# Another order of the projection units in a step of a graph attention kernel

## The reference

```python
h = relu(layernorm(x))
q, k, v = h @ Wq + bq, h @ Wk + bk, h @ Wv + bv          # 12 heads of 32
scores = q @ k^T / sqrt(32) + beta * adj                  # per graph and head, 128 x 128
scores = where(adj > 0, scores, -9e15)
out = x + softmax(scores) @ v
```

## Time and profile before

| | us |
|---|---|
| median of 3 runs | 1061.97 (1061.64 to 1063.23) |
| the profiled execution | 1062.6 |
| its span, first to last instruction | 1060.7 |
| TensorE busy | 1021.5 (96%) |
| TensorE weight loads busy | 710.6 (67%) |
| VectorE busy | 967.8 (91%) |
| ScalarE busy | 878.6 (83%) |
| GpSimd busy | 568.1 (54%) |
| mean granted TensorE clock | 0.987 of full |

### The profile page before, as it was taken

How to read it: one execution, slowest core, us unless ns; L and a number is a source line. 1 busy time by engine, 2 the same in 40 slices (tenths; PEclk the granted TensorE clock), 3 DMA queues, 4 the chain that set the end, 5 groups by cost and what they waited for, 6 DMA issues and landing times. The chain is left out here.

```text
span 1060.7 us, 33776 instructions
## 1 busy us (share of the span) xinstructions
PE 1021.5 (96%) x10959; PEld 710.6 (67%) x10959; DVE 967.8 (91%) x4343; ACT 878.6 (83%) x2343; POOL 568.1 (54%) x756
## 2 busy tenths in 40 slices
PE   3899999999999999999999999999999999999986
PEld 1466676776676776666777666677667677666664
DVE  6579999999999999999999999999999999999887
ACT  3378888888888888888888888888888888888887
POOL 3655655445656445565444565544565644566431
PEclk9899999999999999999999999999999999999997
DMA  4454445544455554445554444555444555445441
GB/s 158 102 132 115 131 131 146 160 131 130 106 138 139 160 138 133 111 131 139 153 144 132 109 139 131 149 149 139 132 111 131 142 160 138 131 105 138 110 121 39
DMA packets 91038, 138.79 MB, mean 131 GB/s; under 512 B 15600, under 2 KB 66288, under 8 KB 90864
## 3 DMA queue, kind: packets, MB, share of 16 engines
q1 hardware_dynamic: 90336, 135.85, 47.6%
q10 hardware_dynamic: 528, 0.79, 0.2%
HBM read 35.91 MB, written 25.17 MB: 58 GB/s over the span
## 5 line engine op out<-in xcount | busy, mean ns | idle before, releaser
L523 ACT ACTIVATE probs<-biased,neg_max 128x128 f32<-128x128 f32 x1536 | 490.3, 391 | 135.9 <-DVE neg_max L638 105.1
L437 PE MATMUL ps_p<-hT,w 128*128 128x512 f16 x1728 | 423.8, 382 | 6.4 <-DVE qT L619 4.2
L638 DVE CUSTOM_DVE_ANT_0 biased<-ps_s,mask 128x128 f32<-128x128 f32 x1536 | 353.4, 286 | 58.7 <-PE ps_s L458 57.0
L336 POOL TENSOR_TENSOR on<-on,xb 128x384 f32<-128x384 f32 x128 | 128.2, 1002 | 363.2 <-DVE on L659 362.4
L437 PEld LDWEIGHTS ps_p<-hT,w 128*128 128x128 f16 x1728 | 167.7, 98 | 158.1 <-DVE hT L609 8.2
L644 DVE TENSOR_TENSOR pT<-ps_t,pT 128x512 f16<-128x512 f32 x384 | 263.3, 686 | 0.9 <-ACT pT L548 0.9
L466 PE MATMUL ps_t<-ident,probs 128*128 128x128 f32 x1536 | 246.2, 283 | 0.1
L548 ACT ACTIVATE pT<-ps_t 128x512 f16<-128x512 f32 x384 | 220.8, 575 | 1.0 <-PE ps_t L466 1.0
L437 PE MATMUL ps_p<-w,hT 128*128 128x384 f16 x1152 | 207.6, 326 | 0.0
L458 PEld LDWEIGHTS ps_s<-k_st,q_st 96*128 96x128 f16 x1536 | 117.9, 97 | 81.4 <-DVE neg_max L638 6.7
L481 PE MATMUL ps_o<-v,pT 128*128 128x33 f16 x1536 | 157.3, 179 | 8.6 <-DVE pT L644 4.9
(11 more groups left out here) (62 smaller groups left out, 1016.9 us busy)
## 6 DMA issues: line engine op xcount, KB each, us to landing
q_st<-qT SPq DMA_DIRECT2D x384, 96.0 KB, 2.2
k_st<-kT SPq DMA_DIRECT2D x384, 96.0 KB, 2.2
out<-on SPq DMA_DIRECT2D x128, 192.0 KB, 2.1
xs<-in_x SPq DMA_DIRECT2D x31, 768.0 KB, 4.8
adjs<-in_adj SPq DMA_DIRECT2D x32, 256.0 KB, 5.1
xs<-in_x ACTq DMA_DIRECT2D x1, 768.0 KB, 7.2
k_st<-in_L_gnn_Wq SPq DMA_DIRECT2D x1, 576.0 KB, 5.4
k_st<-in_L_gnn_Wk SPq DMA_DIRECT2D x1, 576.0 KB, 9.4
```

The lines of the kernel that those rows point to most:

```text
L336: pool.tensor_tensor(on[:, j % 2, :], on[:, j % 2, :], xb[:, par, j, :], ALU.add).then_inc(added, 1)
L437: mm = pe.matmul(dst, stationary, moving, start=m == 0, stop=m == MMS - 1)
L523: act.activation(probs[:, odd, i, :], biased[:, odd, i, :], ACT.Exp, bias=neg_max[:, odd, i:i + 1], scale=-1.0).then_inc(exp_done, 1)
L638: dve.tensor_tensor_reduce(out=biased[:, odd, i, :], in0=ps_s[:, i * N:(i + 1) * N], in1=mask[:, gp, v // CH, :], scale=-1.0, scalar=3.0e3 ...
```

## The change

```diff
-    UNITS = ([("q", c) for c in range(CH)] + [(kind, c) for c in range(CH) for kind in ("k", "turn")]
-             + [("v", j) for j in range(G)])
+    UNITS = ([("q", c) for c in range(CH)] + [("k", 0), ("k", 1), ("turn", 0), ("k", 2), ("turn", 1), ("v", 0), ("turn", 2)]
+             + [("v", j) for j in range(1, G)])
```

## The result

The changed kernel takes 1073.78 us (median of 4 runs, 1073.0 to 1074.72) against 1061.81 before: 1.0111 times as long, 95% interval 1.0098 to 1.0123. The forecast was 1074.3.

What follows compares the result with a forecast made beforehand. It took VectorE's unbroken stretch, bias 7 to `p_low` 9, to bound each step's middle: 0.60 added less 0.20 gained, times 30 steps, is 12.0, plus 0.3 for step 31, on 1061.97 gives 1074.3 us; range 1066 to 1082.

Steps and rivals of the forecast that it cites:

- What bounds the kernel before: Each step: VectorE owns scores 7 to values 10, TensorE the rest; `p_low` waits read as 30, 0.35 us each.
- k2's wait goes, 0.20 us: Slots 5 and 6: k2 no longer waits for t0's low part, so scores 7 come 0.20 us earlier (0 to 0.27).
- A turn's low part more in VectorE's stretch, 0.60 us: Bias 7 to `p_low` 9, without idle time: four low parts instead of three, 0.60 us longer (0.60 to 0.68).
- The step, +0.40: Each of 30 steps ends 0.60 - 0.20 = 0.40 us later, 12.0 us in all; nothing gives it back.
- Inside the stretch: Slots 7 to 10: new stalls of 0.54 us at values 8, 0.12 at t1; none at values 9; 0.33 at values 10.
- Step 31, +0.3: Step without turns: k1's low part comes before `p_low` in slot 7 and stalls values 8, +0.3 us (0 to 0.66).
- What else moves, 0: ScalarE's high parts, SyncE's spread of k, GpSimd and the other banks cause no further wait: cost 0.
- The removed wait decides: Rival: k2's wait goes and VectorE catches up, each step 0.20 us shorter, 1056.0 us; chance 0.07.
- TensorE alone in slot 10: Rival: TensorE's own count decides slot 10, +0.07 us a step, 1064.4 us; chance 0.07 together with a cancelling.
- ScalarE late: Rival: t1's high part delays the exps of slot 8 by 0.58 us, 0.98 a step, 1091.7 us; chance 0.09.
- The clock: Rival: longer pauses of TensorE lower its granted clock, 51 us more if once a step, 1125.3 us; chance 0.03.

Runs made afterwards that it cites:

- e3: Changed kernel with turn t0 put back ahead of k1, so k2 follows k1; 1056.70 us, 0.9953 of before.
- e4: Kernel before with one spare mask-like VectorE instruction (0.66 us) added in slot 7 of 30 steps; 1082.07 us, 1.0204 of before.
- e5: Kernel before with one spare mask-like VectorE instruction added in slot 10 of 30 steps; 1061.68 us, 1.0003 of before.
- e9: Changed kernel with the mask's second part in slot 10 instead of 7 and adj's load behind the spread of k; 1062.69 us, 1.0007 of before.
- e7: Kernel before with the mask's second part in slot 10 instead of 7 and adj's load behind the spread of k; 1048.66 us, 0.9877 of before.
- e2: Changed kernel with the mask's second part in slot 6 instead of slot 7; 1074.98 us, 1.0125 of before.

## Why the prediction was right

**What bounds the kernel before.** Right, read from the timelines. The sum of the earlier trace rows that was given beside them is not: 14 + 16 waits for `p_low` are not one in each of 30 steps, as 25 of them lie behind 1005 us, in the last two steps. That they came to 30, and to 0.35 us each, is chance. The waits of a step are the 0.29 and 0.11 us that were read from the earlier trace rows; over steps 3 to 29 they are 0.30 and 0.11.

**k2's wait goes, 0.20 us.** Right in kind and by 0.02 in size: scores 7 come 5.25 instead of 5.47 us behind scores 5, so 0.22. e3 shows that this gain by itself reaches the end of the step.

**A turn's low part more in VectorE's stretch, 0.60 us.** Right: bias 7 to `p_low` 9 took 516.57 - 509.53 = 7.04 us and takes 523.25 - 515.61 = 7.64. e4 and e5 show that inside the stretch a low part's worth of work costs all of its length, and outside it nothing.

**The step, +0.40.** Measured +0.38: the 0.60 less 0.22.

**Inside the stretch.** Relative to scores 7 the text had t1 at 2.21, values 8 at 3.42, scores 9 at 5.65, scores 10 at 8.39 and values 10 at 8.95; the timeline has 2.21, 3.41, 5.66, 8.40 and 8.94. The stall at values 8 is there (0.48 us, where 0.54 was forecast: t1 takes 0.49 us up to scores 8 and not 0.44), that at values 9 is gone, and bias 10 starts 0.16 us after `p_low` 9 gives way (523.25 + 0.60 against 524.01; 0.15 forecast). Every such place is a sum of start-to-start lengths of one row each, and that is why they add up.

**Step 31, +0.3.** From scores 5 of step 31 to scores 3 behind it 1030.85 - 1007.57 = 23.28 us before, 1043.50 - 1019.92 = 23.58 after: +0.30, and it is there from slot 11 of step 31 on. It can't be found in the whole time, though: at scores 5 of step 32 the two kernels are level (26.68 and 26.69 us behind scores 5 of step 31). In the kernel before the granted clock was 0.50 from 1033 to 1036 us, just there (scores 5 start at 1034.25); in the changed kernel it fell only behind 1050 us (0.66 from 1050 to 1055). So of the 12.3 us forecast, the 30 steps gave 11.5 where 12.0 was put down, and the 0.3 of step 31 is covered by what differs at the end; the medians differ by 11.97.

**What else moves, 0.** Right for ScalarE: nothing in VectorE's stretch waits for a high part, and the exps of slot 8 still wait for VectorE, 0.21 us where it was 0.92. The exps of slot 7 do follow ScalarE's own queue, behind t0's high part, as they followed t1's before, and hold nobody up.

```profile
518.56 0.60 ACT L530 ACTIVATE hT<-ps_p 128x512 f16<-128x512 f32 x1
519.36 1.28 ACT L523 ACTIVATE probs<-biased,neg_max 128x128 f32<-128x128 f32 x4 [0.21 <-DVE neg_max L638]
```

For SyncE it was not quite nothing: the spread of k is waited for twice, 3.3 us, instead of once, 1.5 us, at the start and the end. The start of this one execution is 0.84 us later and its end 0.83 shorter. Other runs of the same order in step 0 had their first scores at 57.69 to 59.32 (58.72 here, 57.87 before), so these ends vary from run to run, and nothing is read from them.

**The rivals.** The removed wait decides: it would have, but for t0 (e3). TensorE alone in slot 10: it does once the mask is out of the stretch (e9: 1062.69, and 1064.4 was its price), not here. ScalarE late: no sign. The clock: granted 1.00 from 60 to 1000 us, with TensorE's busy time down from 934.48 to 925.40 us; the longer pauses did not lower it.

```profile
60.00:1000.00 940.00, 925.40 (x10060) 647.26 (x10059) 876.49 (x3972) 800.81 (x2153) 505.29 (x671) 1.00 0.50 133
```

What the Trainium skill (TensorE: Matmul & The Clock Gate, § A second HAM failure mode: psum-queue depth-cycling) tells of, a clock that goes back and forth while TensorE idles briefly between groups of matmuls, does not show in this trace, with pauses of 0.12, 0.48 and 0.32 us in each step.

## What to carry to other kernels

Where two engines are both over 90% busy, look in each for its stretches without idle time and ask of a moved instruction whether it enters or leaves one: the same instruction cost 20 us in slot 7 and nothing in slot 10. Reordering producers for the sake of one engine's wait also reorders their consumers' work; place each consumer's share of a slot before choosing. And a wait removed shows its worth only when no later wait in the same period takes it up: lay the whole period out from start-to-start lengths before giving it a price.

## What the runs showed of the hardware

A VectorE instruction with two SBUF inputs (L603, 512 float32 elements) takes 0.74 us alone and 1.41 us beside a two-input addition of GpSimd. With that addition moved it has 0.752 us on the mean again. The like instruction of e5, in slot 10 beside GpSimd's split of v, took 1.18 us on the mean against 0.743 in slot 7, and the mask of e7, in the same place, 1.015. A step of e7 has both rows, VectorE's and GpSimd's:

```profile
512.32 1.02 DVE L603 SCALAR_TENSOR_TENSOR mask<-adjs,beta_col,mask 128x512 f32<-128x512 f32 x1
511.90 0.89 POOL L330 TENSOR_TENSOR v<-v_f,v 128x384 f16<-128x384 f32 x1
```

GpSimd's ends at 512.79 and VectorE's at 513.34, 0.55 us later. That holds throughout: in e2, e5 and e7, wherever the mask or the spare instruction starts inside a two-input instruction of GpSimd with over 0.2 us of it left (90 times, with 0.31 to 0.87 us left), it ends 0.545 to 0.553 us after that one, while GpSimd's keeps the length that it has alone (0.88 or 1.00 us). So it isn't slowed in proportion: it is held until the other is nearly done. Its length is what is left of GpSimd's instruction plus 0.55 us.

What the two share is narrower than SBUF as a whole. The low part of q and k (L619), with one input in PSUM and one in SBUF, takes 0.742 us beside GpSimd's two-input additions (58 times in the kernel before) and 0.742 elsewhere. The Trainium skill (VectorE: DVE Perf Modes, § Two Vector instructions with no wait between them) speaks of a second SBUF read interface that VectorE shares with GpSimd and that an instruction with two SBUF inputs reads through. The measured lengths agree with instructions taking turns there, though no run shows the interface itself.
